# A two-layer attention and expert kernel on one core: layer 1's last two batch rows drained by an order of their own

## What is computed

```python
x = x + L0_xattn(layernorm(x), ctx)      # 16 heads of 8 dims, softmax over 128 keys, out-projection
x = x + L0_ffn(layernorm(x))             # top-1 of 8 experts, square(relu(x W1)) W2
x = x + L1_xattn(layernorm(x), ctx)      # as L0, other weights, scores clipped, NaN guard
x = x + L1_ffn(layernorm(x))             # all 8 experts, top-2 gates: sum_e gate[e] * (gelu(x W1[e] + b1[e]) W2[e] + b2[e])
```

## Time and profile before

| | |
|---|---|
| median of 3 runs | 242.50 us (242.43 to 242.52) |
| profiled execution: span, first to last instruction | 242.5 us (no time apart from its span is listed for it) |
| PE busy | 225.4 us (93%) |
| DVE, ACT, POOL busy | 164.2, 121.9, 79.8 us |
| chain that ended last | 68% PE, 17% DVE, 7% DMA |
| layer 1's attention | about 125 to 184 us of the span |
| experts of layer 1 | from about 178.6 us to the end |

### The profile page before, as it was taken

One profiled execution on the slowest core, in us unless ns is written; L12 is line 12 of the kernel. 1 busy time (PEld: TensorE's weight loads), 2 busy tenths in 40 slices (PEclk: granted clock), 3 DMA queues, 4 the chain that ended last, 5 costly groups with the idle time before them and its releaser, 6 DMA issues.

```text
span 242.5 us, 6733 instructions
## 1 busy us (share of the span) xinstructions
PE 225.4 (93%) x2534; PEld 173.1 (71%) x2534; DVE 164.2 (68%) x513; ACT 121.9 (50%) x231; POOL 79.8 (33%) x105
## 2 busy tenths in 40 slices
PE   7999989999998999999987799998999999999993
PEld 7347668776666999998874556777656777766773
DVE  2697668656654865569438675797328974799994
ACT  2653456564674566655600377565435356443340
POOL 8592400001061177745450794564510100000000
PEclk9999999999999999999999999999979999999999
DMA  7990422314014013421122110213000000001001
GB/s 209 392 395 12 118 56 53 90 49 137 3 44 123 0 56 87 135 80 34 44 55 58 45 49 26 69 49 110 27 0 4 0 0 0 3 0 46 3 0 43
DMA packets 12451, 16.38 MB, mean 68 GB/s; under 512 B 1428, under 2 KB 9620, under 8 KB 12292
## 3 DMA queue, kind: packets, MB, share of 16 engines
q1 hardware_dynamic: 10068, 12.87, 17.2%
q0 software_dynamic: 1152, 2.24, 3.2%
q10 hardware_dynamic: 1200, 0.85, 1.1%
HBM read 11.31 MB, written 3.95 MB: 63 GB/s over the span
## 4 chain that ended last, share of the span: by engine, by line
PE 68%; DVE 17%; DMA 7%; issue 3%; POOL 2%; ACT 1%; DVEq 0%; ACTq 0%; SPq 0%; POOLq 0%
PE ps L1240 12%; PE ps L1252 12%; PE ps L1063 10%; PE ps L1108 6%; PE ps L1320 5%; PE ps L1330 5%; DVE mx L681 5%; PE ps L1071 4%; DVE xn L663 4%; PE ps L973 4%; DMA moe_y<-ys,tok_i 3%; DMA work<-moe_y 2%; DVE stats L649 2%; POOL rstd L367 2%; DMA xr<-in_x 2%
## 5 line engine op out<-in xcount | busy, mean ns | idle before, releaser
L681 DVE TENSOR_REDUCE mx<-ps 128x4 f32<-128x512 f32 x64 | 41.0, 685 | 15.6 <-PE ps L1063 15.6
L517 ACT ACTIVATE PT<-ps 128x512 f32<-128x512 f32 x64 | 35.7, 590 | 27.7 <-PE ps L1071 27.7
L1063 PE MATMUL ps<-k,q 32*128 32x128 f32 x512 | 36.1, 282 | 6.8 <-DVE mx L681 5.7
L1063 PEld LDWEIGHTS ps<-k,q 32*128 32x128 f32 x512 | 30.8, 186 | 16.2 <-DVE mx L681 12.9
L1071 PE MATMUL ps<-q,k 32*128 32x128 f32 x512 | 37.2, 283 | 0.0
L1252 PEld LDWEIGHTS ps<-proj,work 128*128 128x128 f32 x256 | 30.7, 192 | 5.7 <-issue 5.7
L627 ACT ACTIVATE work<-ps,fc 128x512 f32<-128x512 f32 x32 | 21.5, 687 | 24.4 <-PE ps L1240 22.9
L1071 PEld LDWEIGHTS ps<-q,k 32*128 32x128 f32 x512 | 31.1, 186 | 1.9 <-issue 1.7
L1240 PE MATMUL ps<-xT,fc 128*128 128x512 f32 x64 | 31.5, 617 | 0.0
L1252 PE MATMUL ps<-proj,work 128*128 128x128 f32 x256 | 31.1, 275 | 0.0
L403 POOL DMA_INDIRECT moe_y<-ys,tok_i x22 | 21.8, 991 | 24.1 <-DVE ys L899 12.0
(11 more groups left out here) (156 smaller groups left out, 314.4 us busy)
## 6 DMA issues: line engine op xcount, KB each, us to landing
proj<-in_proj SPq DMA_DIRECT2D x1, 2048.0 KB, 12.2
fc<-in_fc SPq DMA_DIRECT2D x8, 256.0 KB, 3.3
slots_x<-xs SPq DMA_DIRECT2D x2, 709.5 KB, 12.4
fc<-in_w SPq DMA_DIRECT2D x8, 129.0 KB, 2.3
proj<-in_w SPq DMA_DIRECT2D x8, 128.0 KB, 2.5
wr<-in_wr SPq DMA_DIRECT2D x1, 913.0 KB, 7.9
xs<-slots_x SPq DMA_DIRECT2D x2, 322.5 KB, 3.8
xs<-slots_x SPq DMA_DIRECT2D x2, 258.0 KB, 3.0
```

The costliest lines, as they stand in the source:

```text
L517: nc.scalar.activation(PT[:, j % PTR, :], ps[:, ring_at(layer, ("st", j)), :], ACT.Exp, scale=SCALE).then_inc(b_done, 1)
L681: nc.vector.tensor_reduce(mx[:, b, 4 * g:4 * g + 4], ps[:, S_BANK(layer, j), :].rearrange("p (k m) -> p k m", m=M), axis=AX, op=ALU.max).t ...
L1063: ins = mm(ps[:, S_BANK(layer, 2 * n + i), P * k:P * k + P], q4[r:r + 32, k, L * b:L * b + L], k4[r:r + 32, k, M * b:M * b + M], start=Tru ...
```

## The change

Layer 1's loops now run for 16 steps only (`LAST(layer)`); layer 0's keep 23. What stood in steps 16 to 22 of layer 1 is written out after the loop, on TensorE, VectorE and ScalarE.

- TensorE: `scores_t_row(6)` and `scores_t_row(7)` issue a row's 16 products in one block, going round the four row groups (64, 96, 0, 32), each tile in a bank of its own. The values of a row come as one group of four tiles. `out_proj(0)`'s wait for the last tops becomes a wait for exp 22.
- Banks: the tiles j = 25 to 31 of layer 1 get fixed banks (`ST_BANK`); `out_proj(0)`, `ln_transpose(3, 0)` and the first `expert_up` product share `OUT_A_BANK`; `expert_up` of even and odd experts use other banks than before and wait for the exps that held them (28 and 31).
- VectorE: `norm(16, 4)` stands ahead of `add_and_stats(0)`, `ln_normalise(3, 0)` behind `norm(17, 5)` as before.
- ScalarE: exps 25, 26 and 27 follow each other, `o_evac(5)` behind them; 28 to 30 follow, `o_evac(6)`, 31, then `ln_evac(3, 0)`, `o_evac(7)`, `gate_exp(0)`.
- GpSimd: `rsqrt(3, 0)` moves from ahead of clamp 26 to ahead of clamp 28.

No arithmetic and no DMA is added or taken away.

```diff
@@ -216,7 +216,7 @@
         CONSTS = 7
         SB = lambda l, j: 4 * B * l + j + 1
         BB = lambda l, b: l * B + b + 1
-        y_bank = lambda layer, half: (2, 1 if layer == 0 else 7)[half]
+        y_bank = lambda layer, half: ((2, 1), (OUT_A_BANK, 7))[layer][half]
         VALUE_UNITS = {2 * b + 7: (2 * b, 2 * b + 1) for b in range(5)}
         VALUE_UNITS.update({16: (10, 11), 17: (12,), 18: (13,), 19: (14,), 20: (15,)})
         O_DONE = {2 * b + 7: b for b in range(5)}
@@ -230,12 +230,12 @@
         S_BANK = lambda layer, j: j if layer == 1 and j < 6 else j % 3
         Q_BANK = [[5, 6, 7, 3], [2]]
         V_BANK = [[5, 6], [7, 6]]
-        LN_BANK = [[4, 4], [1, 2], [0, None], [0, 6]]
+        LN_BANK = [[4, 4], [1, 2], [0, None], [None, 6]]
         LG_BANK = (1, 7)
+        LAST = lambda layer: STEPS if layer == 0 else 2 * B
         B2_STEP = {0: ((0, 0),), 1: ((0, 1),), 2: ((0, 2),), 7: ((0, 3), (0, 4)), 8: ((0, 5), (0, 6)), 9: ((0, 7), (1, 0)),
                    10: ((1, 1), (1, 2)), 11: ((1, 3), (1, 4)), 12: ((1, 5), (1, 6)), 13: ((1, 7),)}
         B2_DONE = lambda idx: sum(len(B2_STEP.get(i, ())) for i in range(idx + 1))
-        UP_BANK = ((3, 4), (5, 0))
         DN_BANK = (1, 2)
         ROUTE = 0
         H_BANK, XT_BANK, Y_BANK = (3, 4), 5, 1
@@ -256,6 +256,10 @@
                     RING[1]["ln"] = len(RING[1])
         ring_at = lambda layer, what: 3 + RING[layer][what] % 3
         ring_no = lambda layer, what: len(RING[0]) * layer + RING[layer][what] + 1
+        ST_BANK = lambda layer, j: ({25: 2, 26: 0, 27: 1, 28: ring_at(1, ("st", 26)), 29: ring_at(1, ("st", 24)), 30: 2, 31: 0}.get(j)
+                                    if layer == 1 and j > 24 else ring_at(layer, ("st", j)))
+        OUT_A_BANK = ring_at(1, ("st", 25))
+        UP_BANK = ((OUT_A_BANK, ST_BANK(1, 28)), (ST_BANK(1, 29), ST_BANK(1, 31)))
         XT_NO = lambda k, half: 2 * k + half + 1 - (k == 3)
 
         block = ctx.enter_context(nc.Block())
@@ -433,7 +437,7 @@
                     add_bo(1, 0)
                 if j == 10:
                     add_bo(1, 1)
-                if j == 4 * B - 6:
+                if j == 4 * B - 4:
                     rsqrt(3, 0)
                 pool.wait_ge(b_done, ring_no(1, ("st", j)))
                 nc.gpsimd.tensor_scalar(PT[:, j % PTR, :], PT[:, j % PTR, :], 1.0, FLOOR, ALU.min, ALU.max).then_inc(p_clamp, 1)
...
@@ -562,10 +567,21 @@
                         keys_evac(1, n - 17)
                     if layer == 0 and 20 < n:
                         keys_evac(1, n - 17)
-                    if layer == 1 and n == 19:
-                        ln_evac(3, 0)
-                    if layer == 1 and n == 21:
-                        gate_exp(0)
+                if layer == 1:
+                    exp(24)
+                    top_evac(7)
+                    exp(25)
+                    exp(26)
+                    exp(27)
+                    o_evac(5)
+                    exp(28)
+                    exp(29)
+                    exp(30)
+                    o_evac(6)
+                    exp(31)
+                    ln_evac(3, 0)
+                    o_evac(7)
+                    gate_exp(0)
 
             def gate_exp(half):
                 act.wait_ge(lg1_sub, half + 1)
...
@@ -750,17 +766,25 @@
                         ln_normalise(1, 0)
                     if n in O_T:
                         norm(n, O_T[n])
-                    if layer == 1 and n in (15, 22):
-                        guarded(n // 16)
+                    if layer == 1 and n == 15:
+                        guarded(0)
                     if layer == 0 and n == 18:
                         place(0)
                     if layer == 0 and n == 20:
                         place_experts(0)
-                    if layer == 1 and n == 17:
-                        ln_normalise(3, 0)
-                    if layer == 1 and n == 20:
-                        gate_logits(0)
                 if layer == 1:
+                    norm(16, 4)
+                    add_and_stats(0)
+                    ot(17, 4)
+                    norm(17, 5)
+                    ln_normalise(3, 0)
+                    ot(19, 5)
+                    norm(19, 6)
+                    ot(21, 6)
+                    gate_logits(0)
+                    norm(21, 7)
+                    ot(23, 7)
+                    guarded(1)
                     gate_probs(0)
                     gate_tops(0)
                     gate_values(0)
...
@@ -1068,10 +1093,22 @@
                 def score_t(m, i, k):
                     b, u = divmod(m, 2)
                     r = 32 * ((2 * u + i) ^ FLIP)
-                    ins = mm(ps[:, ring_at(layer, ("st", 2 * m + i)), P * k:P * k + P], k4[r:r + 32, k, M * b:M * b + M],
+                    ins = mm(ps[:, ST_BANK(layer, 2 * m + i), P * k:P * k + P], k4[r:r + 32, k, M * b:M * b + M],
                              q4[r:r + 32, k, L * b:L * b + L], start=True, stop=True, tile_position=(r, 0))
                     if k == 3:
                         ins.then_inc(st_ps, 1)
+
+                def scores_t_row(b):
+                    pe.wait_ge(t_row[b % TRR], 16 * ((BB(1, b) - 1) // TRR + 1))
+                    if b == 6:
+                        pe.wait_ge(b_done, ring_no(1, ("st", 21)))
+                        pe.wait_ge(s_top, SB(1, 4 * B - 1))
+                    else:
+                        pe.wait_ge(b_done, ring_no(1, ("st", 26)))
+                    for k in range(4):
+                        for m in (2 * b, 2 * b + 1):
+                            for i in range(2):
+                                score_t(m, i, k)
 
                 def idle_product(columns):
                     mm(ps[:, 6, 0:columns], ident[:], wcol(0, "wq")[:, 0:columns], start=True, stop=True)
@@ -1132,7 +1169,10 @@
 
                 def out_proj(half):
                     pe.wait_ge(s_wr, 16)
-                    pe.wait_ge(s_top, SB(layer, 4 * B - 3 + half))
+                    if layer == 0:
+                        pe.wait_ge(s_top, SB(layer, 4 * B - 3 + half))
+                    elif half == 0:
+                        pe.wait_ge(b_done, ring_no(1, ("st", 22)))
                     if layer == 0 and half == 1:
                         pe.wait_ge(k_sb, 11)
                     if layer == 0:
...
@@ -1209,16 +1249,30 @@
                         k_proj(1, 5)
                     if layer == 0 and n == 22:
                         k_proj(1, 6)
-                    if layer == 1 and n == 18:
-                        pe.wait_ge(s_top, SB(1, 4 * B - 2))
-                        ln_transpose(3, 0)
-                    if layer == 1 and n == 20:
-                        pe.wait_ge(s_top, SB(1, 4 * B - 1))
-                        gate_scores(0)
-                    if layer == 1 and n == 21:
-                        expert_up(0)
-                    if layer == 1 and n == 22:
-                        expert_up(1)
+                if layer == 1:
+                    scores_t_row(6)
+                    o_transpose(16, 4)
+                    top_transpose(7)
+                    out_proj(0)
+                    for j in range(20, 24):
+                        values(j)
+                    a_transpose(17, 4)
+                    scores_t_row(7)
+                    o_transpose(17, 5)
+                    for j in range(24, 28):
+                        values(j)
+                    a_transpose(18, 5)
+                    ln_transpose(3, 0)
+                    o_transpose(19, 6)
+                    for j in range(28, 32):
+                        values(j)
+                    a_transpose(20, 6)
+                    pe.wait_ge(b_done, ring_no(1, ("st", 27)))
+                    gate_scores(0)
+                    o_transpose(21, 7)
+                    expert_up(0)
+                    a_transpose(22, 7)
+                    expert_up(1)
                 out_proj(1)
 
             def gate_scores(half):
@@ -1231,7 +1285,10 @@
             def expert_up(idx):
                 half, e = divmod(idx, E)
                 if idx == 0:
-                    pe.wait_ge(b_done, ring_no(1, ("st", 4 * B - 1)))
+                    pe.wait_ge(ln_xT, XT_NO(3, 0))
+                    pe.wait_ge(b_done, ring_no(1, ("st", 28)))
+                if idx == 1:
+                    pe.wait_ge(b_done, ring_no(1, ("st", 31)))
                 if idx < E:
                     pe.wait_ge(s_w12[e], 32)
                 if idx >= 2:
```

More of the change, by code:

```diff
@@ L463, in ln_evac @@
                     act.wait_ge(q_ps, 10)
-                nc.scalar.activation(xT[:, 512 * half:512 * half + 512], ps[:, LN_BANK[k][half], :],
+                bank = OUT_A_BANK if (k, half) == (3, 0) else LN_BANK[k][half]
+                nc.scalar.activation(xT[:, 512 * half:512 * half + 512], ps[:, bank, :],
                                      ACT.Copy).then_inc(ln_xT, 1)
@@ L516, in exp @@
                         act.wait_ge(o_ps, SB(layer, j) - PTR)
```

(9 more changed lines are left out.)

## The result

| | before | this |
|---|---|---|
| median of 4 runs each | 242.47 us (242.0 to 242.52) | 240.19 us (239.5 to 240.54) |
| ratio, 95% interval | | 0.990 (0.987 to 0.993) |
| profiled execution: span / own time | 242.5 / not listed | 238.8 / 240.54 us |

The account below looks back on a forecast made before the run. The prediction took TensorE, busy 225.4 of 242.5 us, as the bound; 2.12 + 0.26 + 1.38 + 0.1 - 0.75 = 3.1 us, 4.8 with the clock, gave 237.7 us, range 237.1 to 239.8.

Parts of the forecast that it names:

- against the profiled span of 242.5 us, which is also the median of the three runs: Base of the whole sum: all savings were subtracted from 242.5 us, taken as both profiled span and median.
- the clock's term: TensorE's 3.40 us at 1.2 GHz, from 178.0 to 181.4, would not come: 1.7 us saved.
- the normalise, 1.11 us, to 171.7: VectorE's normalise after row 5's norm would take 1.11 us, ending at 171.7, with TensorE losing 0.6 us.
- scores, 4 blocks to 2: Last transposed scores on TensorE: four blocks of 1.09 us become two of 1.12 us, 2.12 us saved.
- the two waits: TensorE's idles of 0.70 and 0.68 us for VectorE's normalised attention would go: 1.38 us saved.
- transposes, gate products (the rest): Forecast only for a_transpose, costing 0.26 rather than 0.33 us when nothing is waited for: 0.1 us saved.
- new waits: TensorE would lose 0.15 us at row 5's o_transpose and 0.6 ahead of ln_transpose: 0.75 us, bounds 0.3 and 1.1.
- Four row groups bring nothing: Rival: transposed scores in four groups go at the rate of two, 2.1 us missing, 239.8 us; chance 0.03.
- the other estimate of 1.42 us a block: Alternative from the Trainium skill's speedup for a block of 16 score products; the sum would be 0.6 us smaller.
- row 7's maxima: Their DMA would land in time for TensorE, 0 to 0.2 us lost; rival, late and kernel slower, chance 0.02.
- the clamps' cover: GpSimd's last four clamps would end at 172.8, 0.7 us before the last value tile, costing nothing.
- The clock falls again: Rival: thin TensorE work from 171 to 175.2 brings the clock's fall, the 1.7 us are lost, 239.4 us; chance 0.40.

Follow-up runs that it names:

- second group: Follow-up runs sharing one chip, with the kernel before timed beside them; there the kernel before had a median of 242.47 us.
- after_again: The changed kernel run again unchanged: median 240.05 us, ratio 0.989 to the kernel before.
- before_again: The kernel before run again unchanged, on a chip where every kernel took 8 to 9 us longer: median 250.96 us, ratio 0.998.
- two_groups: Changed kernel with each block's same 16 score products issued a tile pair at a time, in two row groups: 249.20 us, ratio 0.992 to the kernel before.
- norm_behind_add: Changed kernel with row 4's norm put back behind add_and_stats(0) on VectorE: 241.71 us, ratio 0.995 to the kernel before.
- before_norm_first: Kernel before with only row 4's norm put ahead of add_and_stats(0) on VectorE: 243.05 us, ratio 1.002 to the kernel before.
- stt_everywhere: Changed kernel with all seven normalises written as scalar_tensor_tensor: 248.81 us, ratio 0.991 to the kernel before.
- stt_normalise: Changed kernel with only layer 1's first normalise written as scalar_tensor_tensor instead of tensor_scalar: 249.35 us, ratio 0.991 to the kernel before.

## Why the prediction was wrong

**First failed step: the sum was made "against the profiled span of 242.5 us, which is also the median of the three runs".** Two different things had the same number. The changed kernel's profiled execution has a span of 238.8 and a time of 240.54, 1.7 us more, and all executions listed have 1.70 to 2.05 between the two. By that an estimate for the profiled execution of the kernel before is 244.2 to 244.6 us, and it was not like the three timed at 242.43 to 242.52. Its mean granted clock was 0.993. In 25 executions of the kernel before in the second group, 17 had a mean granted clock of 0.997 or more and took 241.85 to 242.86 us, median 242.27; 8 had 0.992 or 0.993 and took 243.12 to 244.55, median 243.91. The difference, 1.64 us, agrees with the 1.7 of the earlier trace rows and with the 19.95 - 18.26 = 1.69 us between the two profiled drains. So the clock's term, "**1.7 saved**", was right for the profiled execution and absent from the median it was subtracted from. A mean clock alone doesn't say where the stretch lies: after_again's profiled execution has 0.992 and took 242.17 us, its stretch at 1.2 GHz lies between 7.8 and 11.2 us, and its drain is at full clock. Whether the change makes such executions rarer (8 of 25 before, and of the changed kernel's 11 in the result and after_again only this one) is open. One of the readings that were to bear the 1.7 out was also wrong: the gate scores at 177.19 lay nearly all ahead of the fall at 178.0, and take 0.99 us at full clock in before_again, so only 0.07 of the 0.27 us counted there are the clock's.

**Second failed step: "the normalise, 1.11 us, to 171.7".** In the kernel before the normalise started at 171.60, when the two clamps from 170.34 on had just ended, at 171.55. The move of rsqrt and of the exps put four clamps at 170.71 next to it. Measured 2.19 us and a wait of 1.51, where 0.6 was forecast with bounds of 0.3 to 1.1 on both waits together; with `o_transpose`'s 0.28 for 0.15 it is 1.79 for 0.75. The trace of before had the warning outside the window that was read: the same four pieces took 5.68 us beside memsets at 11.23. The Trainium skill (SBUF — State Buffer, "Who interferes with whom") says that VectorE and GpSimd share one pair of SBUF ports, and that a `tensor_scalar` in a two-port mode contends with GpSimd, an instruction with two SBUF inputs only with a GpSimd instruction that reads SBUF, and one with at most one SBUF input outside those modes not at all. The runs agree with all three: 2.19 us beside clamps and 5.68 beside memsets; 2.36 and 1.14; 1.36 with the source in PSUM. It also says that whoever comes first has the pair for the whole instruction and the other "fully blocks". The single rows agree: each piece of the changed kernel ends 0.07 to 0.08 us behind a clamp's end; beside the memsets the four end in pairs, 0.08 and 0.15 us behind the first memset's end and as much behind the second's; and where a clamp had ended by the first half of a piece (two_groups, norm_behind_add) the piece kept its 0.33 or 0.34 us and the next clamp took 0.69 or 0.70. Who came first the rows don't show, as an instruction's row can begin before the one ahead of it on its engine has ended. So a clamp pays at most 0.08 us, and beside clamps a piece of 0.34 us grew to as much as 0.67 (0.79 in before_norm_first).

The other terms, from the timelines of before_again and after, each block counted from its start to the next start:

| term | forecast | measured |
|---|---|---|
| scores, 4 blocks to 2 | 2.12 | 4.43 - 2.28 = 2.15 |
| values | 0.26 | 2.34 - 2.02 = 0.32 |
| the two waits | 1.38 | 1.38 (0.70 and 0.68, both gone) |
| transposes, gate products (the rest) | 0.1 | 0.33 |
| new waits | -0.75 | -1.79 |
| sum | 3.1 | 2.39 |

242.47 less 2.39 is 240.1, against the 240.19 measured. So the score blocks, the values and the waits removed were right to 0.1 us; the 0.1 for the transposes had the wrong reason, since in the kernel before `a_transpose` takes 0.25 or 0.26 us to the next start with or without a wait ahead of it; "Four row groups bring nothing" is refuted by 1.72 against 1.17 us, and so is the other estimate of 1.42 us a block, though two_groups' blocks, 1.65 us each to the next start, show that only about half of the scores' 2.15 comes from four groups (3.30 - 2.28 = 1.02) and the rest from joining the blocks; row 7's maxima were in time, as there is no idle ahead of its block; the clamps' cover held, since row 7's values didn't wait in the changed kernel. That the time lies nearer to the 239.4 of "The clock falls again" than to the forecast is chance: the clock did not fall in the drain of any of the changed kernel's three profiles. But the rival was a fair one: stt_everywhere's drain, 3.4 us at half clock in it, is 1.55 longer than stt_normalise's. The rows:

```profile
173.00:180.30 7.30, 5.33 (x112) 4.16 (x111) 5.83 (x20) 4.88 (x11) 5.87 (x9) 1.00 0.28 76
180.30:183.70 3.40, 3.40 (x39) 2.58 (x40) 0.67 (x3) 0.64 (x2) 0.00 (x0) 0.50 0.02 5
```

The fall comes behind TensorE's wait of 1.69 us for the normalise; that of norm_behind_add came within a microsecond of its wait of 1.79. The changed kernel has 1.51 at the same place and kept 2.4 GHz, but stt_normalise kept it behind 1.68, and the kernel before lost it behind an idle of 0.68 in one profile and kept it behind the same 0.68 in another, so what decides stays open.

Where the gain went, then: of 4.8 us forecast, 1.7 were never in the median, and 1.04 went into the new waits; the small terms came out 0.3 better. What bounds the changed drain is no longer TensorE's work but the chain `out_proj(0)`, `add_and_stats(0)`, `ot` of row 4, row 5's `o_transpose` and `norm`, normalise, `ln_transpose` (rsqrt ends at 170.74, 0.3 us ahead of that `norm`). Three experiments shortened that chain at the cost of its neighbours and gained 0.1 to 0.2 us. Only the one that took the two engines off each other without delaying either gained 0.8.

## What to carry to other kernels

Before subtracting a term that one profile shows, ask whether the timed runs contain it: compare the profiled execution's own time, not its span, with the median, and where that time isn't listed, say so and give both sums. A duration from a row holds only with its neighbours on the other engines: when VectorE work is moved next to GpSimd work, look for the same instruction beside GpSimd elsewhere in the trace, and if the price is high, let it read PSUM. And a wait that is removed is only a gain if the next one does not hang on the same chain.

## What the runs showed of the hardware

- The same four VectorE pieces (128x128, fp32) took 1.10 us alone, 2.19 beside GpSimd clamps and 5.68 beside memsets of 3.51 and 1.85 us; as `scalar_tensor_tensor` 1.14 beside the first memset and 2.36 beside clamps; reading PSUM 1.36 beside clamps. Beside clamps one piece gets through per clamp, its end 0.07 to 0.08 us behind the clamp's. A clamp of 0.61 us took at most 0.70.
- A block of 16 transposed-score products (32 rows, 128 columns) takes 1.17 us in four row groups and 1.72 in two. Counted to the start of the work behind it, a block of 8 in two groups takes 1.09 and one of 16 in two groups 1.65, so joining two blocks saves 0.5 us without more groups.
- Stretches of 3.4 us at 1.2 GHz come in some executions of a kernel and not in others: 8 of 25 executions of the kernel before had a mean granted clock of 0.992 or 0.993 and took 1.64 us more (median) than the 17 with 0.997 or more.
